# Batch 0's projections in plain fp32, later splits, a first run over a tile of ones and a new merge order in a decoder layer on one core

## The reference, cut to what matters

```python
qkv = hidden_states @ Wqkv                      # 256 -> (16 + 2*2) * 128
xq, xk, xv = heads of qkv; xq, xk = rotary(xq), rotary(xk)
logits = 30 * tanh(xq @ xk.T * SCALE / 30), causal
out = softmax(logits) @ xv @ Wo
x = layernorm(x + out)
x = layernorm(x + xattn(x, ctx));  x = layernorm(x + ffn(x))
```

## Time and profile before

| | |
|---|---|
| median of 3 runs | 399.34 us (399.05 to 400.19) |
| the profiled execution | 399.49 us |
| its span, first to last instruction | 397.8 us |
| TensorE busy | 375.9 us, 94% |
| VectorE busy | 307.3 us, 77% |
| ScalarE busy | 247.7 us, 62% |
| GpSimd busy | 148.9 us, 37% |
| granted TensorE clock, mean | 0.998 |

### The profile page before, as it was taken

The page is one execution under the profiler, slowest core; times in us unless marked ns, Lnnn a source line. Parts: engine busy times, 40 slices in busy tenths (PEclk is TensorE's granted clock), DMA queues, the critical chain, the costliest instruction groups (busy, mean ns, idle before and its releaser), DMA issues.

```text
span 397.8 us, 9280 instructions
## 1 busy us (share of the span) xinstructions
PE 375.9 (94%) x3144; PEld 326.9 (82%) x3144; DVE 307.3 (77%) x924; ACT 247.7 (62%) x528; POOL 148.9 (37%) x173
## 2 busy tenths in 40 slices
PE   3699999999999999999999999999999989899895
PEld 3579799588899887798999878989888888669794
DVE  4999797488677685988887797988788787868643
ACT  4275753445838887466699928589973338983330
POOL 6498856447553331535334113241323211000101
PEclk9999999999999999999999999999999999999999
DMA  7993444934163530233533220122123000000000
GB/s 224 323 375 145 158 136 138 286 81 106 54 169 123 163 79 28 53 108 108 158 93 96 81 54 1 42 92 82 28 81 108 2 0 15 16 2 2 13 16 26
DMA packets 21134, 38.45 MB, mean 97 GB/s; under 512 B 2528, under 2 KB 11616, under 8 KB 21088
## 3 DMA queue, kind: packets, MB, share of 16 engines
q1 hardware_dynamic: 20272, 37.06, 30.5%
q10 hardware_dynamic: 816, 0.79, 0.6%
HBM read 25.52 MB, written 5.24 MB: 77 GB/s over the span
## 4 chain that ended last, share of the span: by engine, by line
PE 82%; DVE 4%; issue 4%; ACT 3%; DMA 3%; POOL 2%; SPq 1%; POOLq 0%; DVEq 0%; ACTq 0%
PE bank L452 14%; PE acc L539 9%; PE bank L506 7%; PE bank L625 7%; PE bank L483 7%; PE bank L677 6%; PE bank L692 4%; PE bank L637 4%; PE bank L614 4%; PE bank L509 3%; PE bank L520 3%; PE bank L491 3%; PE bank L565 2%; DMA rope_s<-rope_t 2%; PE bank L595 2%
## 5 line engine op out<-in xcount | busy, mean ns | idle before, releaser
L831 ACT ACTIVATE xs<-xs,xneg 128x256 f32<-128x256 f32 x128 | 54.5, 499 | 6.1 <-DVE xneg L1089 5.8
L1237 POOL TENSOR_TENSOR q_T<-q_T,rope_s 128x512 f32<-128x512 f32 x24 | 31.0, 1295 | 71.5 <-DMA rope_s<-rope_t 71.4
L452 PE MATMUL bank<-x_hi,wqkv_hi 128*128 128x256 f32 x144 | 44.5, 309 | 8.9 <-DVE wqkv_lo L918 8.9
L1266 POOL TENSOR_TENSOR rstd<-var_eps,half 128x1 f32<-128x1 f32 x24 | 13.2, 550 | 98.5 <-DVE var_eps L976 98.5
L539 PE MATMUL acc<-wo_s,a_hi 128*128 128x256 f32 x256 | 49.8, 293 | 0.0
L1248 POOL TENSOR_TENSOR a_lo<-a_flat,a_hi 128x512 fp32r<-128x512 f32 x32 | 41.3, 1294 | 21.0 <-ACT a_flat L752 20.9
L1089 DVE CUSTOM_DVE_ANT_0 xs<-bank,mask_s 128x256 f32<-128x256 f32 x128 | 46.3, 419 | 2.8 <-PE bank L614 2.6
L452 PE MATMUL bank<-x_lo,wqkv_hi 128*128 128x256 f32 x144 | 41.1, 286 | 0.0
L452 PE MATMUL bank<-x_hi,wqkv_lo 128*128 128x256 f32 x144 | 41.1, 285 | 0.0
L506 PE MATMUL bank<-v_s,p_near 128*128 128x129 f32 x256 | 41.0, 275 | 0.0
L539 PEld LDWEIGHTS acc<-wo_s,a_hi 128*128 128x128 f32 x256 | 39.3, 189 | 1.6 <-issue 1.4
(11 more groups left out here) (152 smaller groups left out, 949.5 us busy)
## 6 DMA issues: line engine op xcount, KB each, us to landing
wo_s<-wo_parts SPq DMA_DIRECT2D x24, 512.0 KB, 3.4
rope_s<-rope_t SPq DMA_DIRECT2D x54, 128.0 KB, 2.3
wo_parts<-wo_s SPq DMA_DIRECT2D x8, 512.0 KB, 3.8
stage<-in_wqkv SPq DMA_DIRECT2D x5, 512.0 KB, 4.7
xs<-in_wo SPq DMA_DIRECT2D x8, 256.0 KB, 4.3
y<-in_x SPq DMA_DIRECT2D x4, 256.0 KB, 2.8
ctx_s<-in_ctxT SPq DMA_DIRECT2D x4, 256.0 KB, 3.4
mask_s<-in_mask SPq DMA_DIRECT2D x4, 256.0 KB, 3.1
```

Source lines behind the costliest of these rows:

```text
L452: ins = mm(ps, lhs[i], rhs[j], start=(k == 0 and n == 0), stop=(last and n == 2))
L831: activation(xs[:, t, m, m2, :], xs[:, t, m, m2, :], ACT.Exp, bias=xneg[:, t, m, m2:m2 + 1], scale=-1.0)\
L1237: g.tensor_tensor(dst, dst, (rope_s if b else rope_t)[:, n % 2], ALU.add).then_inc(sig["rotated", 0], 1)
```

## The change

- In batch 0 the keys, the values and the first four query pairs (pieces 0, 1 and 2: `PLAIN = 3`) are multiplied in fp32 as loaded, from `stage` and `xT_s`, without rounding or splitting; a wait for x and for the piece alone stands before each. Pairs 5 to 8 of batch 0 and all of batches 1 to 3 use the three passes as before.
- All five pieces are still split, for the later use, but later: x and piece 3 after `rot` 2, piece 4 after `rot` 4, pieces 0, 1, 2 after `rot` 6, 7, 8. Each piece has semaphores of its own.
- Pieces 3 and 4 are loaded into `xp_T`, which is free then, so SP issues all loads without a wait. Keys and values come as two loads on ScalarE's queue, ahead of its first instruction.
- TensorE first multiplies a tile of ones by itself seven times, into the accumulator that the first projection overwrites.
- x of batch 1 is loaded by SP at `rot` 5 instead of by ScalarE after the values.
- `ORDER` is a new string. The first `val` and the first `wo` come before the first `rot`.

The core of the diff:

```diff
+WARM = 7
+PLAIN = 3
+SPLITS = ((2, "split_x", 0), (2, "piece", 3), (4, "piece", 4), (6, "piece", 0), (7, "piece", 1), (8, "piece", 2))
...
-    ops = [("split_x", 0)]
-    if b == 0:
-        ops += [("piece", 0), ("piece", 1)]
+    ops = [("split_x", 0)] if b else []
     for i in range(PAIRS + 1):
         ops.append(("rot", i))
-        if b == 0 and i % 2 and i < PAIRS - 1:
-            ops.append(("piece", (i + 3) // 2))
+        if b == 0:
+            ops += [(kind, n) for at, kind, n in SPLITS if at == i]
...
-    "rrrrrrrrmrssmsrmmsrmmmrmssmrrmmmmmrmrsssmmmmmsmmmmsscrmcmmmcmmmmrrccmmmmmmmrrcssmmmmssmrrcmmmmycssmrrmmmm"
+    "mmrrrrrrssrrsmmrsrmmssmmrsmrrmmsmmmsrmmmmrrmmmmcsssmmmmmmrccmmmmrrcmmcmmmmcsmrrmmmmmcsccssrrmmmsmsxmmrrmm"
...
+        spare = xp_T[:].rearrange("p t m a k q -> p (t m a k q)").rearrange("p (s c n) -> p s c n", s=PIECES - PLAIN, c=CK)
+        raw = [*(stage[:, n] for n in range(PLAIN)), *(spare[:, n] for n in range(PIECES - PLAIN))]
...
             sp.dma_start(xT_s[:], rows(xT[0])).then_inc(x_in, 16)
-            sp.dma_start(stage[:, 0], rows(wqkv[:, order[0] * PW:(order[0] + 1) * PW])).then_inc(piece_in[0], 16)
             sp.dma_start(cos_s[:], cos).then_inc(tables_in, 16)
             sp.dma_start(sin_s[:], sin).then_inc(tables_in, 16)
+            for n in range(1, PIECES):
+                sp.dma_start(raw[n], rows(wqkv[:, (n - 1) * PW:n * PW])).then_inc(piece_in[n], 16)
             sp.dma_start(ident_s[:], ident).then_inc(tables_in, 16)
-            for n, c in enumerate(order[1:], start=1):
-                if n >= 3:
-                    sp.wait_ge(piece_lo, 2 * (n - 2))
-                sp.dma_start(stage[:, n % 3], rows(wqkv[:, c * PW:(c + 1) * PW])).then_inc(piece_in[n], 16)
...
+            pe.wait_ge(consts_set, 1)
+            for _ in range(WARM):
+                mm(acc[:, 0, 0:P], ones[:], ones[:], start=True, stop=True, skip_group_check=True)
...
+                        if plain:
+                            r0 = c0 % PW
+                            ins = mm(ps[:, m * T:(m + 1) * T], raw[n][:, k, r0:r0 + HD], xT_s[:, k, :],
+                                     start=(k == 0), stop=(k == CK - 1))
+                            continue
...
+            rows = wqkv.rearrange("(k p) n -> p k n", p=P)
+            act.dma_start(raw[0][:, :, 0:PAIR], rows[:, :, NH * HD:NH * HD + PAIR]).then_inc(piece_in[0], 16)
+            act.dma_start(raw[0][:, :, PAIR:PW], rows[:, :, NH * HD + PAIR:]).then_inc(values_in, 16)
```

More of the change, by code:

```diff
@@ L285, in build_decoder @@
         swapped = [sem(f"swapped{i}") for i in range(2)]
-        piece_hi, piece_lo = sem("piece_hi"), sem("piece_lo")
+        piece_hi = [sem(f"piece_hi{i}") for i in range(PIECES)]
+        piece_lo = [sem(f"piece_lo{i}") for i in range(PIECES)]
         consts_set, bias_scaled = sem("consts_set"), sem("bias_scaled")
@@ L339, in _ @@
             rows = lambda a: a.rearrange("(k p) n -> p k n", p=P)
-            order = [PIECES - 1, *range(PIECES - 1)]
             def load_tokens(b):
@@ L419, in _ @@
                     swap_halves(b, i)
+                elif kind == "rot" and i == 2 * PLAIN - 1:
+                    wait_filled(sp, "rot", 0, 2 * PLAIN - 2)
+                    wait_filled(sp, "val", 0)
+                    wait_for(sp, "x_lo", 0)
+                    sp.dma_start(xT_s[:], rows(xT[1])).then_inc(x_in, 16)
                 elif kind == "quant_w" and i == 1:
@@ L457, in rot @@
                 ps = claim("rot", b, i)
-                wait_for(pe, "x_lo", b)
-                pe.wait_ge(piece_lo, 1 if i == 0 else i + 2)
+                n = (i + 1) // 2
+                plain = b == 0 and n < PLAIN
+                if plain:
+                    pe.wait_ge(x_in, 16)
+                    pe.wait_ge(piece_in[n], 16)
+                else:
+                    wait_for(pe, "x_lo", b)
+                    pe.wait_ge(piece_lo[n], 1 + (i - 1) % 2 if i else 1)
                 for m in range(2):
@@ L468, in val @@
                 ps = claim("val", b)
-                wait_for(pe, "x_lo", b)
-                pe.wait_ge(piece_lo, 2)
+                if b == 0:
+                    pe.wait_ge(x_in, 16)
+                    pe.wait_ge(values_in, 16)
+                else:
+                    wait_for(pe, "x_lo", b)
+                    pe.wait_ge(piece_lo[0], 2)
                 c0 = (NH + NKV) * HD
@@ L473, in val @@
                     for k in range(CK):
+                        if b == 0:
+                            ins = mm(ps[:, t * C:(t + 1) * C], xT_s[:, k, t * P:(t + 1) * P],
+                                     raw[0][:, k, PAIR:PW], start=(k == 0), stop=(k == CK - 1))
+                            continue
                         xk = [a[:, k, t * P:(t + 1) * P] for a in (x_hi, x_lo)]
@@ L771, in val @@
                     .then_inc(sig["values", 0], 1)
-                if b + 1 < B:
+                if b and b + 1 < B:
                     wait_for(act, "x_lo", b)
@@ L847, in hidden @@
                 wait_filled(act, "ffn", b - 1, 0, t)
+                if b == 0:
+                    for n in range(PLAIN):
+                        act.wait_ge(piece_lo[n], 2)
                 n = HT // HPARTS
@@ L915, in split_piece @@
                 for h in range(2):
[L916 removed]
+                    dve.wait_ge(piece_hi[n], h + 1)
                     cols = slice(c * PW + h * PAIR, c * PW + (h + 1) * PAIR)
[L918 to L919 removed]
+                    v.tensor_tensor(wq_lo[:, :, cols], raw[n][:, :, h * PAIR:(h + 1) * PAIR],
+                                    wq_hi[:, :, cols].bitcast(F32), ALU.subtract).then_inc(piece_lo[n], 1)
             def split_x(b):
```

20 lines of the change are left out of this document (10 added, 10 removed).

## The result

The changed kernel takes **404.73 us** (median of 4 runs, 403.99 to 405.80) against 399.37 (399.05 to 400.19): a ratio of 1.0122, 95% interval 1.0104 to 1.0140. Forecast were 398.5 us and a range of 395.0 to 401.5; the result lies 3.2 us outside it, on the other side of no change. Its profiled execution took 403.99 us with a span of 402.2, 4.4 more than before's 397.8. Executions over 1.5% above the fastest of their kernel (one of e6, 466.57 us, two of e12, 404.30 and 404.74, one of e14, 2150.77) are left out of the medians and ratios of this document, and the profiles of e6 and e12 are of such executions.

A forecast was written before the change was run, and what follows sets the result against it. TensorE, busy 94% of the span, was taken as the bound. Span 397.8 - 2.18 (start) + 1.86 (plain fp32) + 0.5 (late splits) - 1.0 (wait near 77 us) = 397.0, giving 398.5 us; range 395.0 to 401.5.

The forecast's parts named there:

- What bounds the kernel: Whole span: TensorE, busy for 94%, carries the chain, so nearly every microsecond lost or added there reaches the end.
- Plain fp32, +1.86 us: TensorE, batch 0: six groups in plain fp32 take 1.73 us each instead of 1.42, adding 1.86 us.
- The ones cost nothing: TensorE's start: seven products of ones fill about 1.1 to 4.1 us, when it had nothing to do.
- First real product 5.2: Start: x and the first weights land so that the first real product starts at 5.2 us, bounds 4.5 and 5.9.
- The first Wo slice lands at 12.2: Start: slice lands at 12.2 us, bounds 11.0 and 15.6; GpSimd's half of it delays keys' rotation, first score tile 16.75.
- VectorE's three steps ... have the keys ready at 10.8: Start: keys' products end at 8.7 us, VectorE's steps finish at 10.8, so GpSimd holds the chain for 3.35 us.
- rival D: Start: TensorE's idle gaps bring the clock down, a second 3.4 us stretch at half speed costs 1.7: 400.2 us; chance 0.14.
- Start, -2.18 us: Until the second score tile ends at 20.25 us: 9.88 us lost instead of 12.06, a gain of 2.18.
- Late splits, +0.5: 25 to 45 us: split subtractions collide with GpSimd's rotations, making VectorE and GpSimd late; +0.5 us, bounds 0 and 1.5.
- The wait near 77 us, -1.0: Batch 1's third score tile comes about 1 us later against the same transfer, removing its wait; bounds 0 and -1.0.
- The last 90 us, 0 with 1 each way: Behind the last projection: nearly the same operations in both orders, so no change, with 1 us allowed each way.
- Rival C: Start: the first Wo slice lands as late as 15.6 us, 3.4 us more, 401.9 us, slower than before; chance 0.14.

The follow-up runs named there:

- e6: The changed kernel without the products of ones at the start (WARM = 0); 402.87 us, ratio 1.0086 to the kernel before.
- e12: The kernel of e8 without the second inner-sum block of batch 0's plain fp32 products (keys, values, queries); 398.65 us, ratio 0.9955 to the kernel before.
- e14: The kernel before the change, with 7 products of ones added ahead of its first product; 399.60 us, ratio 0.9990.
- e4: The changed kernel with 12 products of ones at the start for 7, and 12 more ahead of the first score tile; 402.58 us, ratio 1.0060.
- e5: The kernel before the change, with 12 products of ones added ahead of its first product; 398.41 us, ratio 0.9968.
- e2: The changed kernel with the first Wo slice moved behind the second score tile and fifth rotation, identity left late; 405.59 us, ratio 1.0149.
- e1: The changed kernel with the identity load issued ahead of the four pieces instead of behind them; 404.15 us, ratio 1.0106.
- e3: The changed kernel with both the identity load early and the first Wo slice behind the fifth rotation; 404.42 us, ratio 1.0123.
- e8: The changed kernel with the identity early, 12 products of ones, and the first Wo slice behind the first far cut; 403.63 us, ratio 1.0091.
- e13: The kernel of e11 with the third Wo slice behind the second far cut; 401.37 us, ratio 1.0041 to the kernel before.
- e11: The kernel of e8 with batch 1's third and fourth query products ahead of the context product and first score tile; 402.63 us, ratio 1.0063.

## Why the prediction was wrong, point by point

- **What bounds the kernel** was right in outline: e4's filled gap reaches the end. It doesn't hold at the start. The forecast took it that before's slow first passes cost something; e5's chain shows that the first score tile didn't wait for them, and in e12 4.4 us less work ahead of that tile bring it forward by 1.64.
- **Plain fp32, +1.86 us**: right, slightly low. 0.222 a pass make 1.77 us a group against 1.42, 2.1 us for six. That it reaches the end in full fits e12's median; the rows show it for no more than values and keys.
- **The ones cost nothing**: not contradicted (e6). That seven bring the clock up was true in the traces of after and e2 and not in those of e1 and e3.
- **First real product 5.2**: 6.07, outside the bounds of 4.5 to 5.9. 256 + 512 + 256 KB were taken to arrive as before's had; the values' half on ScalarE's queue came 0.9 us later. It cost nothing behind the gates.
- **The first Wo slice lands at 12.2**: 13.14, within 11.0 to 15.6, but 0.9 us late; keys' rotation 15.16 to 16.43 instead of 14.15 to 15.45. Mechanism right, size off: 1.0 of the 1.45 us by which the first score tile is late (18.20 for 16.75).
- **"VectorE's three steps ... have the keys ready at 10.8"**: a step that failed, though not a dear one. The rope's wait for `tables_in` stands in the list quoted ahead of the forecast, and the diff shows the third load that this semaphore counts move behind the four pieces. I counted the bytes ahead of the Wo slice and not those ahead of the identity in the same queue. It put the ropes at 12.51. With the Wo slice beside it this didn't move the keys (e1). GpSimd, free at 16.43, took the first query at 16.88, released by its rope: the other 0.45 us of the first score tile's lateness.
- **The clock in the gap (rival D)**: **the step that failed and cost most of the start.** The sum took the high clock for all of TensorE's work; the fall was held for unlikely, 0.14, and priced at 1.7 us. It came: the second score tile takes 1.87 us for 0.86, 1.01 more, and the half speed from 22.73 to 24.4 costs about 0.84 more (an estimate, half of those 1.67 us), 1.85 in all. e4, which fills this gap, is 2.1 us faster, of which 1.06 are in place at 30 us, though its tile starts 0.45 later. The forecast had a gap of 2.9 us; it was 3.25. The Trainium skill ("TensorE: Matmul & The Clock Gate", "HAM oscillation") spoke for it, and the trace agrees. I preferred the absence of a fall at before's gaps of 2.1 and 1.1 us, which says nothing on 3; and e1's fall, behind gaps of 1.02 and 1.66, shows that the longest gap alone doesn't decide.
- **Start, -2.18 us**: +0.30 by the end of the second score tile (12.36 - 12.06), and +1.6 by 60 us with plain fp32 left out (3.45 - 1.86). This is the largest miss, 3.3 us against -2.18 + 0.5. By the end of the second score tile it is 2.48 us (22.73 for 20.25): 1.46 for its late start (20.86 for 19.4) and 1.01 for the clock; then come the 0.84.
- **Late splits, +0.5**: the collisions came as described (1.75 us for a subtraction at 19.60, 1.76 for a rotation at 19.04). The Trainium skill's rule in "SBUF — State Buffer" ("SBUF: two separate sides") agrees with both. I looked for their cost at the turns; it lay in GpSimd's list ahead of the far cuts: waits of 0.29 us in after (at 30.75), and of 0.53 and 1.46 us in e8, the latter of which e13 removes.
- **The wait near 77 us, -1.0**: **the other step that failed, in its sign.** TensorE's wait of 0.97 us there didn't go. It became two, of 0.75 at 72.52 and 0.47 at 85.02, and one of 0.65 at 90.05 for a far cut came with them. The first stands behind the second pair's exchange, issued at 67.33 against 60.81 before:

```profile
72.52 1.10 PE L513 MATMUL bank<-q_T,k_T 128*128 128x512 f32 x2 [0.75 <-POOL q_T L1276]
```

  the others behind the third pair's, issued later too and longer, in the chain of after (against 71.75 and 4.63 us in the earlier trace rows):

```profile
77.38 6.10 DMA rope_s<-rope_t
```

  I had let TensorE's side of the meeting move and kept the transfer's date fixed. The term came out at +1.2 (60 to 300 us), a miss of 2.2.
- **The last 90 us, 0 with 1 each way**: -0.28, right.
- **Rival C** gave 401.9 with a mechanism that didn't occur (a slice at 15.6; it landed at 13.14). Each rival was priced alone, and the range ended short of C. C and D together, 3.4 + 1.7 above 398.5, would have been 403.6.

The misses add up: 3.3 (start and what follows to 60 us) and 2.2 (middle), less 0.3 behind, 5.2 us, which is the distance between the forecast change of the span, -0.82, and the measured 4.4.

## What to carry to other kernels

When a load moves in a queue, look up every counter that it feeds and every instruction that waits on that count, not only those that read its tile: a semaphore shared by three loads makes the last of them a gate for all. When a repair of the start makes the first tile sooner, look at the in-order lists of the helping engines: what was moved out of the way has to stand somewhere, and here it stood before the next tile's cut. When a wait depends on a transfer that the kernel itself issues, both sides move with the change. And where a change leaves TensorE a new gap, add up the sum at both clock levels before the lower one is called unlikely: here the fall was the dearest part of the start.

## What the runs showed of the hardware

- A gap of 3.25 us on TensorE behind 8.9 us of unbroken work brought the granted clock to 0.50 from within the gap until 24.4 us. In e1 it fell behind gaps of 1.02 and 1.66 us with one score tile between them. It stayed at 1.00 over 1.54 us in e4, and after a gap of 2.46 us in e5 (15.05) the passes still stood 0.12 apart.
- Seven products of ones that end 2.5 us ahead of real work left the passes at 0.21 us until 12.45 (e14), 2.2 us longer than no ones at all (10.27). With seven ones ahead of plain fp32 the first eight passes took 3.75 us in e3 (1.29 us after the ones) and e1 (1.72), and 1.97 in e2 (1.19) and after (1.84): the gap's length doesn't sort them. The 12 that reach up to the first product gave full speed in e5 and e8, and in e4 but for the first passes (2.34 us for eight). In these runs only ones that reached the start could be counted on.
- A VectorE subtraction and a GpSimd addition that overlap are both longer: 1.75 us and 1.76 in after at 19 to 21 us, for 0.69 (x's subtraction of the same shape, at 18.99) and 1.27.
- A DMA of 64 KB issued at 4.27 behind some 3 MB landed 8.14 us later. The transfer of exchanged halves (128 KB a piece) took 3.1 us in a quiet stretch (e11, at 65.62) and 6.1 to 7.1 beside a Wo reload and the loads of context and x.
